# The experts of a graph network's last layer in 105 tiles of 128 places instead of 56 tiles of 256

## The reference, cut to what matters

```
def _L1_ffn_ref(x, Wg, bg, W1, b1, W2, b2):
    xf = x.reshape(-1, D)                              # 6250 x 256
    top_w, top_i = jax.lax.top_k(xf @ Wg + bg, 2)      # two of 8 experts for each node
    top_w = jax.nn.softmax(top_w, axis=-1)
    w_dense = jnp.sum(jax.nn.one_hot(top_i, 8) * top_w[..., None], axis=1)
    out = jnp.zeros_like(xf)
    for e in range(8):
        h = jax.nn.gelu(xf @ W1[e] + b1[e], approximate=False)      # 1024 hidden
        out = out + w_dense[:, e:e + 1] * (h @ W2[e] + b2[e])
```

## Time and profile before

| | us |
|---|---|
| median of three executions | 4050.02 (4049.96 to 4054.22) |
| the profiled execution, first to last instruction | 4484.1 |
| of it: from the experts' first transpose to the end | 3811.9 to 4484.1 |
| the same, TensorE's last matmul | 4467.8 |

### The profile page before, as it was taken

One profiled execution on the slowest core, in us unless ns is written; L12 is line 12 of the kernel. 1 busy time (PEld: TensorE's weight loads), 2 busy tenths in 40 slices (PEclk: granted clock), 3 DMA queues, 4 the chain that ended last, 5 costly groups with the idle time before them and its releaser, 6 DMA issues. The chain is left out here.

```text
span 4484.1 us, 71720 instructions
## 1 busy us (share of the span) xinstructions
PE 2615.8 (58%) x17373; PEld 1754.5 (39%) x17374; DVE 2381.6 (53%) x7860; ACT 977.5 (22%) x2424; POOL 2086.9 (47%) x2286
## 2 busy tenths in 40 slices
PE   2534455555566572899993333343333332999997
PEld 1422333343444461344442222232222221776775
DVE  6433444454555567777773445455555556455554
ACT  1300001111122222566660000000000112333332
POOL 1566666565555521000006666666666620455554
PEclk9866666677778785899996666666666665999998
DMA  3232222222222211344444444444333316222222
GB/s 111 92 88 82 84 83 77 73 78 69 69 66 67 71 28 38 131 206 187 201 192 148 131 131 137 128 135 127 90 92 94 92 47 222 41 47 46 47 47 36
DMA packets 170312, 440.84 MB, mean 98 GB/s; under 512 B 41488, under 2 KB 95888, under 8 KB 163744
## 3 DMA queue, kind: packets, MB, share of 16 engines
q0 software_dynamic: 101984, 250.24, 21.2%
q1 hardware_dynamic: 60528, 183.32, 10.8%
q10 hardware_dynamic: 7760, 6.83, 0.5%
HBM read 283.78 MB, written 156.47 MB: 98 GB/s over the span
## 5 line engine op out<-in xcount | busy, mean ns | idle before, releaser
L718 POOL DMA_INDIRECT g_msg<-table,g_idx x1664 | 1623.1, 975 | 637.0 <-issue 507.4
L782 PE MATMUL psum<-g_msg,g_hot 128*128 128x256 f16 x1664 | 569.4, 342 | 992.8 <-issue 992.3
L737 DVE TENSOR_SCALAR g_hot<-iota,g_cols 128x128 f16<-128x128 f16 x3328 | 779.0, 339 | 69.1 <-issue 39.2
L782 PEld LDWEIGHTS psum<-g_msg,g_hot 128*128 128x128 f16 x1664 | 201.0, 121 | 1101.8 <-issue 1049.2
L783 PE MATMUL psum<-g_msg,g_hot 128*128 128x256 f16 x1664 | 568.1, 341 | 47.0 <-issue 46.7
L784 PE MATMUL psum<-g_msg,g_hot 128*128 128x256 f16 x1664 | 564.7, 339 | 51.6 <-issue 51.5
L1264 DVE SCALAR_TENSOR_TENSOR t_row<-psum,t_gate,t_row 128x256 f16<-128x256 f32 x800 | 350.3, 480 | 153.2 <-ACT t_row L1307 153.2
L1307 ACT ACTIVATE t_row<-psum,t_gate 128x256 f16<-128x256 f32 x800 | 336.1, 471 | 185.0 <-PE psum L1340 185.0
L733 DVE CAST g_cols<-step_cols 128x24 f32 x208 | 41.9, 202 | 548.7 <-remote 282.1
L1657 POOL DMA_INDIRECT out<-ex_y,ex_to x112 | 207.7, 1854 | 248.6 <-DMA out<-ex_y,ex_to 167.8
L1339 PE MATMUL psum<-wrel_lo,t_xhi 128*128 128x512 f16 x800 | 304.1, 380 | 0.0
(11 more groups left out here) (361 smaller groups left out, 4926.8 us busy)
## 6 DMA issues: line engine op xcount, KB each, us to landing
table<-t_row SPq DMA_DIRECT2D x50, 2048.0 KB, 6.3
g_msg<-table,g_idx POOLq DMA_INDIRECT x1664
piece_stage<-in_w SPq DMA_DIRECT2D x32, 512.0 KB
w_halves<-piece_halves SPq DMA_DIRECT2D x32, 512.0 KB
w<-w_halves SPq DMA_DIRECT2D x8, 2048.0 KB, 22.5
rows<-sc_row ACTq DMA_DIRECT2D x52, 128.0 KB
acc<-in_x SPq DMA_DIRECT2D x5, 1280.0 KB, 13.6
table<-t_row SPq DMA_DIRECT2D x25, 256.0 KB, 2.1
```

The costliest lines, as they stand in the source:

```text
L718: pool.indirect_dma_start(out=msg[b * BATCH + k][:, :], out_offset=None, in_=table, in_offset=bass.IndirectOffsetOnAxis(ap=idx[b][:, k:k + ...
L737: last = nc.vector.tensor_scalar(hot[b][:, (2 * k + h) * P:(2 * k + h + 1) * P], t["iota16"][:, :], c3[:, k, LOCAL - first:LOCAL - first + ...
L782: pe.matmul(ps, hi, row[:, 0:D], start=False, stop=False, skip_group_check=True)
```

## The change

Tiles of 128 places: 2 x 6,250 and at most 127 empty places for each expert make 105 tiles. Each engine does for 128 places what it did for 256. On TensorE the 48 matmuls of `up` move 128 columns instead of 256, those of `down` are 16 instead of 32, and the transposes 4 instead of 8. The halves `g`, `ghi`, `glo` are held twice, and the hidden layer has two sets of two banks, so that tile n+1 waits for tile n-1 instead of n; `y` is held four times. GpSimd's loop is gone: its 105 tiles are written out with constant columns of `node_at` and `node_to` as the DMAs' offsets, without copies. The loops of the other engines have 25 rounds of four tiles and five tiles behind them. `shares` has two instructions instead of three.

```
-SUBS = 2
-TOKENS = SUBS * P
+TOKENS = P
 PLACE_TILES = (NODES * TOP + EXPERTS * (TOKENS - 1)) // TOKENS
-PLACE_TILES += PLACE_TILES % 2
...
-    g, ghi, glo = w.sb("ex_g", [P, HC * TOKENS], F32), w.sb("ex_ghi", [P, HC * TOKENS], F16), w.sb("ex_glo", [P, HC * TOKENS], F16)
+    g, ghi, glo = pair("g", HC * P, F32), pair("ghi", HC * P, F16), pair("glo", HC * P, F16)
...
-    psT, psH, psY = core.bank[0:2], core.bank[2:6], core.bank[6:8]
-    BANKS = len(psH)
     DEPTH = 2
+    HALF = 2
+    psT, psH, psY = core.bank[0:2], [core.bank[2:4], core.bank[4:6]], core.bank[6:8]
+    PER = HC // HALF
...
-            def fetch(n, b):
-
-                core.hold(pool, "pool", turned, n + 1)
-                core.hold(pool, "pool", share_done, n + 1)
-                pool.tensor_copy(idx[b][:, :], t["node_at"][:, n * SUBS:(n + 1) * SUBS] if isinstance(n, int) else
-                                 t["node_at"][:, bass.ds(n * SUBS, SUBS)]).then_inc(idx_done, 1)
-                core.hold(pool, "pool", idx_done, n + 1)
-                for s in range(SUBS):
-                    pool.indirect_dma_start(out=xin[b][:, s * ROW:(s + 1) * ROW], out_offset=None, in_=dram["rows"],
-                                            in_offset=bass.IndirectOffsetOnAxis(ap=idx[b][:, s:s + 1], axis=0)).then_inc(x_in[b], 16)
...
+            def fetch(n):
+
+                pool.wait_ge(turned, n + 1)
+                pool.wait_ge(share_done, n + 1)
+                pool.indirect_dma_start(out=xin[n % AHEAD][:, :], out_offset=None, in_=dram["rows"],
+                                        in_offset=bass.IndirectOffsetOnAxis(ap=t["node_at"][:, n:n + 1], axis=0)).then_inc(x_in[n % AHEAD], 16)
+
+            def add(n):
+
+                pool.wait_ge(added, 16 * (n + 1))
                 pool.sem_inc(y_free, 1)
...
+                pool.wait_ge(y_done, n + 1 + AHEAD)
+                pool.indirect_dma_start(out=out, out_offset=bass.IndirectOffsetOnAxis(ap=t["node_to"][:, n:n + 1], axis=0),
+                                        in_=y[n % AHEAD][:, :], in_offset=None, compute_op=ALU.add).then_inc(added, 16)
...
             def up(n, b):
                 e = owner(pe, n)
                 pe.wait_ge(xT_done, n + 1 + DEPTH)
-                for j in range(BANKS):
-
-                    pe.wait_ge(gelu_done, BANKS * n + j + 1)
-                    for c in (2 * j, 2 * j + 1):
-                        out = psH[j][:, (c % 2) * TOKENS:(c % 2 + 1) * TOKENS]
+                for j in range(HALF):
+
+                    pe.wait_ge(gelu_done, HALF * n + j + 1)
+                    for c in range(PER * j, PER * (j + 1)):
+                        to = psH[b % 2][j][:, (c % PER) * P:(c % PER + 1) * P]
                         for k in range(KC):
                             at = (k * HC + c) * 2 * P
                             whi, wlo = (w1[:, bass.ds(e * KC * H * 2 + (at + h * P), P)] for h in range(2))
-                            hi, lo = (xT[b % 2][:, (h * KC + k) * TOKENS:(h * KC + k + 1) * TOKENS] for h in range(2))
...
+                            hi, lo = (xT[b % 2][:, (h * KC + k) * P:(h * KC + k + 1) * P] for h in range(2))
...
             def down(n, b):
                 e = owner(pe, n)
-                pe.wait_ge(y_done, SUBS * (n + AHEAD))
-                pe.wait_ge(glo_done, n + 2)
+                pe.wait_ge(whole_done, n + 1)
+                pe.wait_ge(glo_done, n + 1 + DEPTH)
...
-                    for s in range(SUBS):
...
+                    hi, lo = (x[b % 2][:, c * P:(c + 1) * P] for x in (ghi, glo))
```

More of the change, by code:

```diff
@@ L1590, in experts @@
     AHEAD = 4
[L1591 to L1594, removed]
+    xin = [w.sb(f"ex_xin{b}", [P, ROW], F32) for b in range(AHEAD)]
+    mine = [w.sb(f"ex_mine{b}", [P, TOP], F32) for b in range(AHEAD)]
+    share = [w.sb(f"ex_share{b}", [P, 1], F32) for b in range(AHEAD)]
@@ L1595, in experts @@
+    y = [w.sb(f"ex_y{b}", [P, D], F32) for b in range(AHEAD)]
     none = w.sb("ex_none", [P, D], F32)
     place_no = w.sb("ex_place_no", [P, PLACE_COLS], F32)
-    xT = pair("xT", 2 * KC * TOKENS, F16)
-    g, ghi, glo = w.sb("ex_g", [P, HC * TOKENS], F32), w.sb("ex_ghi", [P, HC * TOKENS], F16), w.sb("ex_glo", [P, HC * TOKENS], F16)
[L1599 to L1602, removed]
+    xT = pair("xT", 2 * KC * P, F16)
@@ new lines, in experts @@
+    g, ghi, glo = pair("g", HC * P, F32), pair("ghi", HC * P, F16), pair("glo", HC * P, F16)
+    sum_, whole = pair("sum", D, F32), pair("whole", D, F32)
+    turned, xT_done, up_done, gelu_done, ghi_done, glo_done, down_done, sum_done, whole_done, y_done, numbered, mine_done, share_done, added, y_free, none_made = core.sems(*(
+        f"ex_{k}" for k in ("turned", "xT_done", "up_done", "gelu_done", "ghi_done", "glo_done", "down_done", "sum_done", "whole_done", "y_done",
+                            "numbered", "mine_done", "share_done", "added", "y_free", "none_made")))
@@ L1660, in _ @@
-            for n in range(AHEAD):
[L1661 to L1668, removed]
+            pool.sem_inc(y_free, AHEAD - 1)
+            def fetch(n):
[3 more added lines that the diff above has]
+                                        in_offset=bass.IndirectOffsetOnAxis(ap=t["node_at"][:, n:n + 1], axis=0)).then_inc(x_in[n % AHEAD], 16)
@@ new lines, in add @@
+            def add(n):
+                pool.wait_ge(added, 16 * (n + 1))
+                pool.sem_inc(y_free, 1)
+                pool.wait_ge(y_done, n + 1 + AHEAD)
+                pool.indirect_dma_start(out=out, out_offset=bass.IndirectOffsetOnAxis(ap=t["node_to"][:, n:n + 1], axis=0),
+                                        in_=y[n % AHEAD][:, :], in_offset=None, compute_op=ALU.add).then_inc(added, 16)
+            for n in range(AHEAD):
+                fetch(n)
+            for n in range(N):
+                if n + AHEAD < N:
+                    fetch(n + AHEAD)
+                add(n)
@@ L1696, in shares @@
-                nc.vector.tensor_tensor(both(mine[b]), facts[:, :, TOP:2 * TOP], here.unsqueeze(2).to_broadcast([P, SUBS, TOP]),
-                                        ALU.is_equal).then_inc(mine_done, 1)
-                dve.wait_ge(mine_done, 2 * n + 1)
-                nc.vector.tensor_tensor(both(mine[b]), both(mine[b]), facts[:, :, 0:TOP], ALU.mult).then_inc(mine_done, 1)
-                dve.wait_ge(mine_done, 2 * n + 2)
-                nc.vector.tensor_reduce(share[b][:, :], both(mine[b]), AX.X, ALU.add).then_inc(share_done, 1)
+                facts = xin[b][:, D:ROW]
@@ new lines, in shares @@
+                core.hold(dve, "dve", turned, n + 1 + AHEAD)
+                dve.wait_ge(y_done, n + 1)
+                nc.vector.scalar_tensor_tensor(out=mine[b][:, :], in0=facts[:, TOP:2 * TOP], scalar=col(place_no, n), in1=facts[:, 0:TOP],
+                                               op0=ALU.is_equal, op1=ALU.mult).then_inc(mine_done, 1)
+                dve.wait_ge(mine_done, n + 1)
+                nc.vector.tensor_reduce(share[b][:, :], mine[b][:, :], AX.X, ALU.add).then_inc(share_done, 1)
@@ L1729, in _ @@
             shares(0, 0)
-            split(0)
+            split(0, 0)
             slots(dve, slot)
@@ L1761, in _ @@
             copy(0, 0)
-            gelu(0)
+            gelu(0, 0)
             copy(1, 1)
@@ L1805, in down @@
                     both, whi = w2[:, bass.ds(at, 2 * D)], w2[:, bass.ds(at, D)]
[L1806 to L1813 removed]
+                    hi, lo = (x[b % 2][:, c * P:(c + 1) * P] for x in (ghi, glo))
+                    if c < HC - 1:
+                        pe.matmul(ps[:, :], hi, both, start=c == 0, stop=False)
+                        pe.matmul(ps[:, 0:D], lo, whi, start=False, stop=False)
+                    else:
+                        pe.matmul(ps[:, 0:D], lo, whi, start=False, stop=False)
+                        pe.matmul(ps[:, :], hi, both, start=False, stop=True).then_inc(down_done, 1)
             def slot(n, b, left):
```

117 lines of the change are left out of this document (45 added, 72 removed).

## The result

The changed kernel takes 4161.11 us (median of 4 runs, 4159.22 to 4162.98), the kernel before 4050.60 in the same job. The ratio is 1.0273 with a 95% interval of 1.0259 to 1.0287: slower, by 110 us.

The account below looks back on a forecast made before the run. TensorE's sequencer was taken as the new bound: 105 x 7.3 = 767 us plus 13 for start and end, 780 against 672, +108 in the profiled execution. Taken near that sum, 4050 + 110 = 4160 us, range 4070 to 4215.

Parts of the forecast that it names:

- Sequencer as the new bound: Experts' stage: TensorE's sequencer needs 7.3 us for 128 places, above the engine's 5.5; register instructions step at 0.125 us.
- The engine's own 5.5 us: TensorE's matmuls for 128 places: `down` 2.6, `up` 2.7, transposes 0.2, sum 5.5 us, x 105 = 578.
- engine bound: Rival: the sequencer isn't the bound in the experts' stage; 591 us, a gain of 54 to 81, about 3985; chance 0.13.
- Owner reads at 1.0 and 1.1 us: TensorE's sequencer, each tile: reading the owner and waiting takes 1.0 us before `up` and 1.1 before `down`.
- `place` and `invert`, put at nothing: Ahead of the experts: `place` and `invert` change their width by some per cent, counted as nothing.
- What the profile would show: Signs in the experts' stage: 210 owner loads, `up` matmuls 0.083 apart, TensorE idle 1 us before `down`, last chain through its sequencer.
- signs of being wrong: `up` matmuls 0.056 apart behind register instructions; adds back to back with TensorE waiting for rows; or stretches at 0.5 clock.
- GpSimd, double sets at nothing: Experts' stage: GpSimd, at 4.7 to 5 us for 128 places, leaves the chain; the double sets cost nothing.
- Weight loads: Rival: 99 ns loads don't hide in `up`; a tile takes 7.6 us, +139, about 4190; chance 0.04.
- clock: Rival: TensorE's clock falls in the experts' stage, up to 1.7 us a tile, 4200 to 4330; chance 0.07.
- From the profiled execution to the runs: Profiled execution 434 us above the median: +135 if the stage lost share to GpSimd's DMAs, +34 to +61 if profiling slows the sequencer.
- The break-even: Experts' stage: the change turns faster below 5.9 us a tile; near 5.9 to 6.0 no change, chance 0.04.

Follow-up runs that it names:

- e2: The changed kernel with TensorE taking every tile's weights from expert 0's constant address, without owner reads or register instructions: 3976.26 us, ratio 0.9825.
- e3: The kernel before, tiles of 256, with TensorE taking every tile's weights from expert 0's constant address: 4042.39 us, ratio 0.9988.
- e4: The changed kernel with the owner read for `up` kept in its register for `down` of the same tile, five reads in four tiles instead of eight: ratio 1.0126.
- e7: The changed kernel with GpSimd's part as before, a loop of four tiles and copies of the indices: ratio 1.0235.
- e8: The changed kernel with one set of g, ghi, glo and one set of two PSUM banks for `up` instead of two: ratio 1.0241.
- e9: The changed kernel with each `up` written eight times with constant addresses, chosen by three branches on the owner: 4745.95 us, ratio 1.1725.
- e1: The kernel before, unchanged, profiled again: 4477.13 us in one run, beside runs of 4481.32 on that chip.

## Why the prediction was right

**Sequencer as the new bound.** Right. Forecast 7.3 us a tile, measured 7.25 by the same rows; step 0.125, measured 0.124 to 0.125; stage 780, measured 782.1. e2 and e3 show it by removal, in the changed kernel and in the one before. One reading in it does not hold: the step "looks like the register instruction's own duration", but the earlier trace rows give 46 ns for that. What fills the rest of the step is not shown.

**The engine's own 5.5 us.** Right: e2 runs at 5.50. Its stage of 600.3 against the 591 of the rival "engine bound" misses by 9, in start and end.

**Owner reads at 1.0 and 1.1 us.** These included the waits around them; the read alone is 0.72 (e4). That the stage came out within 2 us is in part luck. From transpose to transpose a tile is 7.22, so the tiles are 758 us for the 767 of the sum, and start and end are 24 for its 13. `place` and `invert`, put at nothing, are 6 us shorter: from `place`'s first matmul to the experts' first transpose 88.4 us before (3723.44 to 3811.86) and 82.6 after (3293.82 to 3376.43). With them the profiles give 104.6 us for the change, the runs 110.5; the difference is not explained.

**What the profile would show.** The 210 loads, GpSimd's wait for y and the clock are as written. The chain is not: it runs through TensorE's matmuls, with 10.3% of "issue", where the sequencer was named. One of the signs of being wrong is there, too: the first 24 matmuls of `up` start 0.056 apart, and the mean over an `up` is (3811.61 - 3808.27) / 47 = 0.071 us, not 0.083. It doesn't speak against the sequencer: that is ahead by what it issued during `down`, the second half runs at its 0.083, and the engine stands ahead of the next `down`. TensorE is idle ahead of `down` for 0.7 us in most tiles (75.6 us in 102), less than the 1 us named, and its busy share is 664 of 740, 90%, not "well below" 97: the drawn length of a matmul covers the gaps in `up`.

**GpSimd, double sets at nothing.** Right in the changed kernel (e7, e8). The prediction did not ask what GpSimd's part alone would give the kernel before: 16 us.

**Weight loads, clock.** Neither happened. Pauses of 0.7 us before each `down` left the clock at 1.00; with the longer ones of e9 it was 0.77. In e2 matmuls of 128 columns start 0.056 us apart, each with a weight load of its own. The Trainium skill (TensorE: Matmul & The Clock Gate, Back-to-back issue gap) gives some 81 ns for such a pair, so the measured number stands.

**From the profiled execution to the runs.** The worry was mistaken, and with it the larger part of the chance for "faster". The 434 us were looked for in the profiler; 429 of them are between the first gather pass and `place` (3531 us for 3102), outside the changed stage. The later profiles show that the stage doesn't follow the chip: e3's on the quick chip, 664 with constant weights, is 8 us from e1's on the slow one, and e8's on a slow chip, 782.4 with single sets, is that of the changed kernel, 782.1. The middle value of +110 came out right because it took the plain sum, not because of this step.

**The break-even.** It was given as 5.9 us a tile. By the prediction's own terms it is (645 - 13) / 105 = 6.0 to (672 - 13) / 105 = 6.3; this changes no measured reading.

## What to carry to other kernels

Where addresses come from registers, count what the engine's sequencer has to do for each tile and set it beside the engine's own time: a smaller tile halves the engine's work for each instruction and none of the sequencer's. The busy row and the chain don't show that limit; the starts of register instructions do. Count the reads that bring an address into a register first: here two of them weighed 1.44 us of a tile, as much as a dozen register instructions. Before a bound is lifted, look for the wait that stands next to it (here ScalarE's copy behind its gelu, 0.75 us a tile away), and try a change's parts alone: one of three was worth keeping, in the kernel that the change replaced.

## What the runs showed of the hardware that I had not expected

- A branch of TensorE's sequencer in the tree of e9 took 0.22 us in the median and up to 4.8, and with the tree in the loop 6.34 MB of instructions were fetched where the changed kernel fetched 0.25.
- A read of one number into a register of TensorE's sequencer, with its bounds instructions, costs 0.72 us and is hidden by nothing when the sequencer is the limit (e4).
- The same program takes 4050 us on one chip and 4480 on another. Of the 434 us between the profiled execution of before and its runs, the stretch from the first gather pass to `place` has 429 when set beside the changed kernel's profile; the experts' stage hardly differs.
